# State-space layer of a four-layer kernel: residual added by the output product, normalization sums on ScalarE, an order of units changed

## The reference

```
h   = layernorm(xn) * g + b                    # 256 channels
xi, z = split(h @ W_in.T)                      # 512 channels each
u   = silu(causal conv over 4 tokens of xi)
dt, B, C = split(u @ W_x.T);  dt = softplus(dt @ W_dt.T + b_dt)
state[t] = exp(dt*A) * state[t-1] + dt*u*B     # 512 channels x 16 states
y   = (sum over states of state*C + u*D) * silu(z)
x   = x + (xn + y @ W_out.T)
```

## Time and profile before

| what | value |
|---|---|
| median of three runs | 2292.87 us |
| the profiled execution | 2300.35 us |
| its span | 2298.60 us |
| TensorE, VectorE, ScalarE, GpSimd busy in the span | 84%, 74%, 52%, 62% |
| the state-space layer's scans | 1081.7 to 1983.8 us |

### The profile page before, as it was taken

The page is one execution under the profiler, slowest core; times in us unless marked ns, Lnnn a source line. Parts: engine busy times, 40 slices in busy tenths (PEclk is TensorE's granted clock), DMA queues, the critical chain, the costliest instruction groups (busy, mean ns, idle before and its releaser), DMA issues. The chain is left out here.

```text
span 2298.6 us, 32626 instructions
## 1 busy us (share of the span) xinstructions
PE 1941.0 (84%) x9846; PEld 1136.6 (49%) x9846; DVE 1694.2 (74%) x2406; ACT 1198.6 (52%) x2466; POOL 1430.1 (62%) x1164
## 2 busy tenths in 40 slices
PE   2499999999873999947989898989898987569998
PEld 1234444444433999933444444444444433257776
DVE  4488777787744656522999999999999999655654
ACT  1066666666652433325676767676767574223222
POOL 7334435543342444422999999999999999444444
PEclk9699989898876999978999999999999999879999
DMA  3554444453143544424040404040404040101110
GB/s 81 103 110 101 103 96 108 111 124 100 51 153 127 100 70 75 76 39 157 0 148 19 148 19 148 19 148 19 148 19 148 10 148 9 60 7 37 36 36 19
DMA packets 231216, 185.57 MB, mean 81 GB/s; under 512 B 148729, under 2 KB 201601, under 8 KB 231058
## 3 DMA queue, kind: packets, MB, share of 16 engines
q1 hardware_dynamic: 216178, 162.61, 25.1%
q0 software_dynamic: 13296, 17.77, 4.4%
q10 hardware_dynamic: 1584, 3.24, 0.4%
HBM read 134.07 MB, written 49.49 MB: 80 GB/s over the span
## 5 line engine op out<-in xcount | busy, mean ns | idle before, releaser
L1769 POOL TENSOR_TENSOR mb_dbu<-mb_dtu,mb_bbc 128x1024 f32<-128x1024 f32 x256 | 600.4, 2361 | 41.8 <-DVE mb_hp L1900 29.6
L473 ACT ACTIVATE ex_plain<-at_t_ps 128x512 f32<-128x512 f32 x512 | 289.4, 595 | 185.9 <-PE at_t_ps L851 180.7
L1902 DVE TENSOR_TENSOR_SCAN mb_da_ps<-mb_da_ps,mb_dbu 128x1024 f32<-128x1024 f32 x160 | 365.3, 2283 | 12.6 <-ACT mb_da_ps L1819 12.6
L1953 PE MATMUL mb_y_ps<-mb_hc,lw_ident 128*128 128x512 f32 x640 | 323.9, 631 | 57.2 <-DVE mb_hc L1908 57.2
L610 DVE TENSOR_REDUCE at_mx<-at_s_ps 128x2 f32<-128x1024 f32 x256 | 310.8, 1219 | 51.4 <-PE at_s_ps L860 49.1
L860 PE MATMUL at_s_ps<-ex_w 48*128 48x512 f32 x512 | 228.1, 507 | 38.4 <-DVE at_mx L610 24.9
L851 PE MATMUL at_t_ps<-ex_w 64*128 64x512 f32 x512 | 221.7, 490 | 12.6 <-ACT ex_plain L473 6.7
L1953 PEld LDWEIGHTS mb_y_ps<-mb_hc,lw_ident 128*128 128x128 f32 x640 | 123.7, 199 | 215.7 <-issue 127.0
L1775 POOL TENSOR_TENSOR mb_hp<-mb_hp,mb_cbc 128x1024 f32<-128x1024 f32 x96 | 226.6, 2361 | 0.0
L1211 POOL DMA_INDIRECT x<-m_o,m_xs x71 | 113.7, 1602 | 172.8 <-DMA x<-m_o,m_xs 111.5
L1900 DVE TENSOR_TENSOR_SCAN mb_hp<-mb_da_ps,mb_dbu 128x1024 f32<-128x1024 f32 x96 | 218.8, 2279 | 2.5 <-ACT mb_da_ps L1819 2.5
(11 more groups left out here) (317 smaller groups left out, 4107.7 us busy)
## 6 DMA issues: line engine op xcount, KB each, us to landing
mb_bbc<-mb_scr SPq DMA_DIRECT2D x64, 512.0 KB, 5.4
mb_cbc<-mb_scr SPq DMA_DIRECT2D x64, 512.0 KB, 4.7
ex_w<-at_scr SPq DMA_DIRECT2D x384, 64.0 KB, 2.3
m_xs<-rt_rows SPq DMA_DIRECT2D x71, 129.0 KB
at_scr<-at_qk_hi SPq DMA_DIRECT2D x32, 256.0 KB
at_scr<-at_qk_lo SPq DMA_DIRECT2D x32, 256.0 KB
at_xin<-in_x SPq DMA_DIRECT2D x32, 128.0 KB, 2.3
ex_plain<-in_x SPq DMA_DIRECT2D x8, 512.0 KB
```

Source lines behind the costliest of these rows:

```text
L473: act.activation(probs[:, c, h, :], t_ps[:, k % 2, :], ACT.Exp, scale=SCALE).then_inc(exp_done, 1)
L1769: pool.tensor_tensor(dbu[:, q % 3, :, :], dtu_2, bbc[:, 2 * p:2 * p + 2, :], ALU.mult).then_inc(S["dbu_ready"], 1)
L1902: dve.tensor_tensor_scan(da, da, add, 0.0, ALU.mult, ALU.add).then_inc(S["scan_done"], 1)
L1953: last = pe.matmul(y_ps[:, v % 2, :], ident[:, :], src[:, j, :], start=False, stop=(q == tile_last[v] and j == 1))
```

## The change

The output product of a token tile begins with identity times the residual rows, so that PSUM holds the sum; ScalarE copies it to `res` two slots after the product, where VectorE added it three slots after. The statistics of a batch are now taken by ScalarE tile by tile, in slots 10 to 13 of the table instead of all in slot 11: a copy scaled by 1/256 with a sum over the row (the mean), a copy of the mean times -1/16, and the square of x/16 - mean/16 with a sum over the row (the variance). What the two wide instructions write goes to `res` and is overwritten later by norm_r. They wait for the store of the batch that last used this part of `res`. In the table xi 1 moves from slot 0 of the next batch to 31, xi 0 from 31 to 30, z 3 from 26 to 24 and both tr from 27 to 26; the tables of the first two batches keep the earlier order, except that xi 1 of the second batch stands in slot 1. `POOL_UNITS` names the same units as `POOL_PAIRS` did.

```diff
--- before.py
+++ after.py
@@ -1621,22 +1621,22 @@
 NP = DS // 2
 NU = ND * NP
 
-POOL_PAIRS = (1, 3, 5)
+POOL_UNITS = tuple(q for q in range(NU) if q % NP in (1, 3, 5))
 
 SCHEDULE = {
-    0: [("xi", 1, 1)], 1: [("dt", 1, 0)], 2: [("out_a", 0, -1)], 3: [("out", 0, -1)], 4: [("out_a", 1, -1)], 5: [("out", 1, -1)],
-    6: [("conv_a", 0, 1), ("final", 0, 0)], 7: [("conv", 0, 1)], 8: [("dt", 2, 0), ("load", 0, 2)], 9: [("conv_a", 1, 1)], 10: [("conv", 1, 1)],
-    11: [("xi", 2, 1), ("ln", 0, 2)], 12: [("xi", 3, 1)], 13: [("z", 0, 1), ("newton", 0, 2)], 14: [("conv_a", 2, 1), ("final", 1, 0), ("rsqrt", 0, 2)],
+    1: [("dt", 1, 0)], 2: [("out_a", 0, -1)], 3: [("out", 0, -1)], 4: [("out_a", 1, -1)], 5: [("out", 1, -1)],
+    6: [("conv_a", 0, 1), ("final", 0, 0)], 7: [("conv", 0, 1)], 8: [("dt", 2, 0), ("load", 0, 2)], 9: [("conv_a", 1, 1)], 10: [("conv", 1, 1), ("ln", 0, 2)],
+    11: [("xi", 2, 1), ("ln", 1, 2)], 12: [("xi", 3, 1), ("ln", 2, 2)], 13: [("z", 0, 1), ("ln", 3, 2), ("newton", 0, 2)], 14: [("conv_a", 2, 1), ("final", 1, 0), ("rsqrt", 0, 2)],
     15: [("conv", 2, 1)], 16: [("dt", 3, 0)], 17: [("conv_a", 3, 1), ("norm_r", 0, 2)], 18: [("conv", 3, 1)], 19: [("silu_u", 0, 1)],
-    20: [("norm_h", 0, 2)], 21: [("z", 1, 1)], 22: [("xd", 0, 1), ("final", 2, 0)], 23: [("z", 2, 1)], 24: [("scr", 0, 1), ("bb", 0, 1), ("bb", 1, 1)],
-    25: [("dt", 0, 1), ("bb", 2, 1), ("cb", 0, 1)], 26: [("z", 3, 1), ("bb", 3, 1), ("cb", 1, 1)], 27: [("tr", 0, 2), ("tr", 1, 2), ("bb", 4, 1), ("cb", 2, 1)],
-    28: [("silu_z", 0, 1), ("bb", 5, 1), ("cb", 3, 1)], 29: [("bb", 6, 1), ("cb", 4, 1)], 30: [("final", 3, 0), ("bb", 7, 1), ("cb", 5, 1)],
-    31: [("xi", 0, 2), ("cb", 6, 1), ("cb", 7, 1)],
+    20: [("norm_h", 0, 2)], 21: [("z", 1, 1)], 22: [("xd", 0, 1), ("final", 2, 0)], 23: [("z", 2, 1)], 24: [("scr", 0, 1), ("z", 3, 1), ("bb", 0, 1), ("bb", 1, 1)],
+    25: [("dt", 0, 1), ("bb", 2, 1), ("cb", 0, 1)], 26: [("tr", 0, 2), ("tr", 1, 2), ("bb", 3, 1), ("cb", 1, 1)], 27: [("bb", 4, 1), ("cb", 2, 1)],
+    28: [("silu_z", 0, 1), ("bb", 5, 1), ("cb", 3, 1)], 29: [("bb", 6, 1), ("cb", 4, 1)], 30: [("xi", 0, 2), ("final", 3, 0), ("bb", 7, 1), ("cb", 5, 1)],
+    31: [("xi", 1, 2), ("cb", 6, 1), ("cb", 7, 1)],
 }
-LATER = (("z", 0, 1), ("z", 1, 1), ("z", 2, 1), ("z", 3, 1), ("norm_h", 0, 2), ("silu_z", 0, 1))
-MOVED = {24: LATER[4:5], 25: LATER[0:2], 26: LATER[2:4]}
-EARLY_SCHEDULES = {-1: {at: [task for task in SCHEDULE[at] if task not in LATER] + list(MOVED.get(at, ())) for at in SCHEDULE},
-                   0: {at: SCHEDULE[at] + [("silu_z", 0, 0)] * (at == 1) for at in SCHEDULE}}
+MOVED = {24: [("norm_h", 0, 2)], 25: [("z", 0, 1), ("z", 1, 1)], 26: [("z", 2, 1), ("z", 3, 1)], 27: [("tr", 0, 2), ("tr", 1, 2)], 31: [("xi", 0, 2)]}
+LATER = [task for at in MOVED for task in MOVED[at]] + [("xi", 1, 2), ("silu_z", 0, 1)]
+EARLY_SCHEDULES = {-1: {at: [task for task in SCHEDULE[at] if task not in LATER] + MOVED.get(at, []) for at in SCHEDULE},
+                   0: {at: [("xi", 1, 1)] * (at == 1) + SCHEDULE[at] + [("silu_z", 0, 0)] * (at == 1) for at in SCHEDULE}}
 FILL_KINDS = ("out", "z", "dt", "tr", "xi", "conv", "xd")
 
 
@@ -1650,7 +1650,7 @@
         zero1 = sb("zero1", [P, 1])
         xin = sb("xin", [P, 4, D])
         res = sb("res", [P, 3, 4, D])
-        stats, mv = sb("stats", [P, 4, 6]), sb("mv", [P, 4, 2])
+        mv, nm = sb("mv", [P, 4, 2]), sb("nm", [P, 4])
         av, lv, rs, tv, nb = (sb(q, [P, 2, 4]) for q in ("av", "lv", "rs", "tv", "nb"))
         up = sb("up", [P, 4])
         hT_hi, hT_lo = (sb(f"hT_{s}", [P, 2, T], F32R) for s in ("hi", "lo"))
@@ -1669,7 +1669,7 @@
         y_ps = ctx.enter_context(nc.psum_tensor("mb_y_ps", [P, 2, T], F32))
         f_ps = ctx.enter_context(nc.psum_tensor("mb_f_ps", [P, 2, T], F32))
 
-        names = """prep a_exp x_stored const_set x_loaded stats_done var_ready a_made ln_done rs_ready
+        names = """prep a_exp x_stored const_set x_loaded stats_done a_made ln_done rs_ready
                    newton norm_ready h_ready f_ready hT_hi_ready z_ready u_ready scr_written ex_steps ex_ready dt_steps dtu_ready
                    da_ready dbu_ready scan_done hc_ready hp_ready y_summed yg_ready"""
         S = {q: sem("mb_" + q) for q in names.split()}
@@ -1699,11 +1699,11 @@
             eng.wait_ge(f_used[k % 2], k // 2 + 1)
 
         def by_pool(q):
-            return q % NP in POOL_PAIRS
+            return q % NU in POOL_UNITS
 
         def turn(q):
 
-            return sum(by_pool(v) == by_pool(q) for v in range(q % NP)) + (q // NP) * (len(POOL_PAIRS) if by_pool(q) else NP - len(POOL_PAIRS))
+            return sum(by_pool(v) == by_pool(q) for v in range(q % NU)) + (q // NU) * (len(POOL_UNITS) if by_pool(q) else NU - len(POOL_UNITS))
 
         def multiplied(eng, q):
 
@@ -1818,8 +1818,16 @@
                         act.activation(da_ps[:, q % 2, 0, :], dt[:, d % 2, :], ACT.Exp, scale=a_neg[:, d, 2 * p:2 * p + 1])
                         act.activation(da_ps[:, q % 2, 1, 1:T], dt[:, d % 2, 1:T], ACT.Exp, scale=a_neg[:, d, 2 * p + 1:2 * p + 2]).then_inc(S["da_ready"], 1)
                     for kind, i, m in tasks(s - 2):
+                        if kind == "ln":
+                            act.wait_ge(S["x_loaded"], 16 * (m + 1))
+                            wait(act, S["x_stored"], 16 * (m - 2))
+                            act.activation(res[:, m % 3, i, :], xin[:, i, :], ACT.Copy, scale=1.0 / D, accum_out=mv[:, i, 0:1]).then_inc(S["stats_done"], 1)
+                            act.wait_ge(S["stats_done"], 12 * m + 3 * i + 1)
+                            act.activation(nm[:, i:i + 1], mv[:, i, 0:1], ACT.Copy, scale=-1.0 / 16.0).then_inc(S["stats_done"], 1)
+                            act.wait_ge(S["stats_done"], 12 * m + 3 * i + 2)
+                            act.activation(res[:, m % 3, i, :], xin[:, i, :], ACT.Square, scale=1.0 / 16.0, bias=nm[:, i:i + 1], accum_out=mv[:, i, 1:2]).then_inc(S["stats_done"], 1)
                         if kind == "rsqrt":
-                            act.wait_ge(S["var_ready"], m + 1)
+                            act.wait_ge(S["stats_done"], 12 * m + 12)
                             act.activation(av[:, 0, :], mv[:, :, 1], ACT.Identity, bias=fix[:, 0:1]).then_inc(S["a_made"], 1)
                             act.activation(av[:, 1, :], mv[:, :, 1], ACT.Identity, scale=1.0 + 1e-6, bias=fix[:, 1:2]).then_inc(S["a_made"], 1)
                             act.wait_ge(S["a_made"], 2 * m + 2)
@@ -1862,6 +1870,9 @@
                                     last = act.activation(z[:, part[0]:part[1], :], z[:, part[0]:part[1], :], ACT.Silu)
                             last.then_inc(S["z_ready"], 1)
                             act.preload_act_table_set("natural_log_exp_and_others")
+                        if kind == "out":
+                            f, used = filled(act, "out", i, m)
+                            act.activation(res[:, m % 3, 2 * i:2 * i + 2, :], f.rearrange("p (a c) -> p a c", a=2), ACT.Copy).then_inc(used, 1)
                         if kind == "xd":
                             f, used = filled(act, "xd", 0, m)
                             wait(act, S["scr_written"], 16 * m)
@@ -1912,15 +1923,6 @@
                             dve.wait_ge(S["y_summed"], tile_summed[v])
                             dve.wait_ge(S["z_ready"], m + 1)
                             dve.tensor_tensor(u[:, m % 2, i, :], y_ps[:, v % 2, :], z[:, v % 5, :], ALU.mult).then_inc(S["yg_ready"], 1)
-                        if kind == "ln":
-                            dve.wait_ge(S["x_loaded"], 16 * (m + 1))
-                            wait(dve, S["h_ready"], m)
-                            for k in range(4):
-                                dve.bn_stats(stats[:, k, :], xin[:, k, :]).then_inc(S["stats_done"], 1)
-                            dve.wait_ge(S["stats_done"], 4 * m + 4)
-                            for k in range(4):
-                                last = dve.bn_aggr(mv[:, k, :], stats[:, k, :])
-                            last.then_inc(S["var_ready"], 1)
                         if kind == "tr":
                             f, used = filled(dve, "tr", i, m)
                             dve.wait_ge(S["hT_hi_ready"], 2 * m + i + 1)
@@ -1934,10 +1936,6 @@
                             dve.tensor_tensor(f, lg[:, :], f, ALU.subtract).then_inc(S["dt_steps"], 1)
                             dve.wait_ge(S["dt_steps"], 2 * v + 2)
                             dve.tensor_tensor(dt[:, i % 2, :], f, dt[:, i % 2, :], ALU.add).then_inc(used, 1)
-                        if kind == "out":
-                            f, used = filled(dve, "out", i, m)
-                            r_2 = res[:, m % 3, 2 * i:2 * i + 2, :]
-                            dve.tensor_tensor(r_2, f.rearrange("p (a c) -> p a c", a=2), r_2, ALU.add).then_inc(used, 1)
 
             @block.tensor
             def _(pe):
@@ -1985,8 +1983,9 @@
```

(3 more changed lines are left out.)

## The result

The changed kernel takes 2294.95 us (median of 20 runs, 2290.14 to 2299.07) where the kernel before takes 2291.55 (20 runs): ratio 1.0015, 95% interval 1.0008 to 1.0022. That is +3.4 us (the interval gives 1.8 to 5.0), slower than before by less than 0.2%; the forecast was +9.0.

What follows compares the result with a forecast made beforehand. VectorE was taken as the bound, with ScalarE and TensorE touching it at a few places. Terms beside the scans (+0.9) and outside (+8.1) summed to +9.0 us, giving 2301.9 us; range 2286 to 2312.

Steps and rivals of the forecast that it cites:

- first gate product, six batches: Second to seventh batch: extra output products on TensorE make each first gate product 0.53 us later, +3.2 us.
- second gate product: Statistics leaving VectorE gain 1.53 us in five batches, 1.73 in the first; the seventh loses 0.2: together -9.2 us.
- fourth gate product: In six batches the new order adds 2.7 us of TensorE work, exceeding the slack: +10.1 us, bounds nothing and 13.
- first scan to first gate product: First batch: xi 1 stands before dt 1 and the gate function in ScalarE's queue, where VectorE already waits: +0.6 us.
- first statistics: Before the scans, on the only path: ScalarE's four tiles take 5.4 us instead of VectorE's 1.7, +3.7 us.
- second statistics: Between conv 1 and the gate function: 5.4 us of sums less ScalarE's 2.7 us wait for TensorE, +2.7 us.
- Before the scans: Ahead of the first scan nothing covers ScalarE's sums, so two batches' statistics cost +3.7 and +2.7 us.
- sign that I named for a wrong forecast: First scan starting less than 3 us later, or VectorE's waits at the fourth gate product being absent.
- (a): Projections hide at the fourth gate product because the half-clock spell is short: the 10.1 us go, 2291.8; chance 0.2.
- (b): Modelled matmul ends hide larger slack at the first and fourth gate products: some -10 us, 2282.8; chance 0.13.
- (c): ScalarE's read-outs dear, 1.8 us a tile, and a longer half-clock spell on TensorE: +10 us, 2312; chance 0.17.
- (d): Moving z 3 two units sooner does nothing, running in TensorE's idle time at the bank: costed at nothing; no chance given.

Runs made afterwards that it cites:

- e1: The changed kernel with the order of units put back as before; sums on ScalarE and residual on TensorE stay: 2284.84 us, ratio 0.9973.
- e2: The kernel before with only the statistics sums moved to ScalarE; order and residual as before: 2280.71 us, ratio 0.9956.
- e5: The changed kernel with z 3 and both tr back in their earlier slots; only xi 0 and xi 1 sooner: 2290.69 us, ratio 0.9994.
- e6: The changed kernel with xi 0 and xi 1 back in their earlier slots; only z 3 and tr sooner: 2291.87 us, ratio 0.9998.
- e7: The changed kernel with the residual added by VectorE as before, without identity products or ScalarE's copies: 2289.43 us, ratio 0.9990.
- e10: The changed kernel with the first two batches' statistics back on VectorE: 2294.33 us, ratio 1.0004.
- e4: The kernel before with only the new order of units; statistics and residual stay on VectorE: 2305.35 us, ratio 1.0065.
- e8: The kernel before with sums on ScalarE only for the six batches beside the scans; the first two stay on VectorE: 2281.46 us, ratio 0.9949.
- e11: The kernel of e8 measured once more, nothing changed: 2281.87 us, ratio 0.9947 to the kernel before.

## Why the prediction was partly right

The direction was right, and so was the place of nearly every gain and loss. The size was wrong: the sum, +9.0, was 4.1 us above the layer's +4.93 and 5.6 above the medians' +3.4. The time lies in the range; of the two outcomes that 0.2% separates, "same" came, which had 0.22. By the prediction's own terms:

| term | forecast | measured |
|---|---|---|
| first gate product, six batches | +3.2 | 6 x 0.56 = +3.4 |
| eighth batch | -1.2 | -1.2 |
| second gate product | -9.2 | -10.3 |
| small waits at the third | -2.6 | -3.1 |
| fourth gate product | +10.1 | +8.9 |
| first scan to first gate product | +0.6 | +1.7 |
| first statistics | +3.7 | +3.2 |
| second statistics | +2.7 | +2.1 |
| from there to the first scan | nothing | -1.4 |
| end | +1.7 | +1.6 |
| sum | +9.0 | +4.9 |

**The step that failed** is the one of "Before the scans": "there nothing covers ScalarE", +3.7 and +2.7. It took ScalarE's delay to reach the first scan at its full length. Forecast +6.4, measured +3.9. Of the 2.5 us between them 1.1 are sizes: a tile was 0.08 us cheaper, VectorE's first statistics had held the path 1.9 us instead of 1.7 (1019.51 to 1021.45 in the trace of before), and the second sums delayed the gate function by 2.1 us. The other 1.4 us are a term that I put at nothing: TensorE's clock on the path from the gate function to the first scan. The eight instructions of xd, the table of stretches, before and after:

```profile
1057.67:1063.86 6.19, 6.18 (x8) 1.41 (x8) 0.00 (x0) 1.16 (x1) 0.00 (x0) 0.58 0.00 0
1052.33:1057.76 5.43, 5.43 (x8) 1.29 (x8) 0.00 (x0) 1.15 (x1) 0.00 (x0) 0.66 0.00 0
```

The same work takes 6.19 us at a granted clock of 0.58 and 5.43 at 0.66, and the z projections behind it take 0.7 us less as well (0.63 and 0.72). The change edits neither. This is not one execution's chance: in the six kernels with the first sums on ScalarE (after, e1, e2, e5, e6, e7) TensorE stands idle 6.1 us before xd, xd takes 5.09 to 5.44 us and the first scan comes 25.6 to 26.0 us after the gate function's table load; in the seven others it is idle 4.4 us, xd takes 6.19 to 6.43 and the distance is 27.4 to 27.7. Why the clock is higher after the longer wait was not tried. So, against before, the sums cost 5.2 - 1.9 us at the first batch, 1.6 to 2.1 at the second, and 1.4 to 1.8 come back on the way to the first scan. e10 gives the part of the sums as a whole, 3.5 us. Within one kind the starts still differ by up to 1 us (69.02 to 70.00, 66.05 to 66.68).

With that step two others were mis-sized: the fourth gate product 1.2 us too dear and the second 1.1. A term of 1.1 us was missing on the other side, below; that it nearly cancels the 1.4 us is luck.

**The fourth gate product.** The added work, +2.7 us at the full clock, was right to the tenth. The slack I set against it was the mean over the batches of before, and contains their spells (27.2 us in six); after had 25.2, which is 1.0 of the 1.2 us that I was too high. The upper bound of 13 us, for longer spells, was right in kind and in size: e4, with the same order and spells that are 5.4 us longer in sum than before, pays 12.7 us there.

**The second gate product.** The forecast of -1.53 a batch was -1.66 in four batches and -2.03 in the fifth, and nothing was lost in the seventh, where I had put +0.2.

**First to first.** In the first batch xi 1 ahead of dt 1 costs VectorE 0.6 us, as forecast (e4 and e10: +0.57). In after another 1.1 us comes with the sums, a wait of 1.00 at the gate product among it. It is TensorE's clock again. After its last wait before this product TensorE has the same instructions in after and in e10; timeline and table of stretches, after first:

```profile
1101.01 3.78 PE L1951 MATMUL mb_y_ps<-mb_hc,lw_ident 128*128 128x512 f32 x4 [3.83 <-DVE mb_hc L1919]
1104.58 3.19 PE L1974 MATMUL mb_f_ps<-mb_xi,lw_diag 128*128 128x512 f32 x4
1104.00:1107.00 3.00, 3.00 (x4) 1.08 (x4) 2.90 (x3) 1.39 (x3) 3.00 (x3) 0.50 0.02 5
...
1102.54 3.45 PE L1964 MATMUL mb_y_ps<-mb_hc,lw_ident 128*128 128x512 f32 x4 [3.83 <-DVE mb_hc L1923]
1105.82 1.88 PE L1987 MATMUL mb_f_ps<-mb_xi,lw_diag 128*128 128x512 f32 x4
1105.54:1108.54 3.00, 3.00 (x8) 1.32 (x8) 2.90 (x3) 1.39 (x3) 3.00 (x3) 1.00 0.00 0
```

The wait is the same 3.83 us, but the convolution behind it takes 3.19 us at 0.50 instead of 1.88 at 1.00. The lower clock lasts 5.9 to 6.2 us here in the three kernels that have both the first sums on ScalarE and xi 1 sooner (after, e5, e7) and 2.9 to 3.4 in the ten others, and only those three wait at this gate product.

**What the profile was to show.** L1940 and the statistics are gone from VectorE, and a tile is 1.27 us (1.3 to 1.5 named). The aside that cheaper tiles would lower the sum by 1.5 us was too small: before the scans the sum holds eight tiles, so 0.25 to 0.45 us off each make 2.0 to 3.6. VectorE's wait at the gate product is 21.2 us (about 26 named, though the parts named beside it and the last wait make 25.2): 1.00 and six of 1.66 at the first, none at the second where I named five, six of 0.68 to 1.35 at the fourth, 3.8 at the end. TensorE's wait at the transposes is 6.7 us a batch (7.6), and the first scan comes 3.9 us later (6). Neither sign that I named for a wrong forecast appeared.

**Rivals.** (a), the projections hide, fell: the waits at the fourth gate product are there in all six batches. It nearly holds for either move alone (0.2 us there in e5, 0.9 in e6). (b), modelled ends hide a larger slack, fell: waits begin where the modelled slack ends, at 0.03 to 0.04 us, and interval less half the spell is 27.5 within 0.03 us over 18 batches. (c), dear read-outs and longer spells, fell for this kernel with 1.27 us a tile; its longer spell, which costs 3 us there, is real in e4 (2.7). (d) stays open: z 3 was moved only together with the transposes, never alone.

## What to carry to other kernels

Taking work off the bounding engine pays by the slack of the next one at that place: the same 1.2 us a batch were worth nothing with 0.36 us of slack behind them and 1.2 us where a convolution was missing, and the 1.73 us of the statistics were worth all of it. Slack is shared: two moves that cost 0.2 and 2.7 us alone cost 8.8 together, so measure a bundle's parts both alone and removed. And place decides for the lender too: sums on ScalarE are free beside the scans and cost 3.5 us before them, where nothing runs beside. A later start of the same products can also meet another clock: a delay of 5.3 us before the first scan arrived there as 3.9.

## What the runs showed of the hardware

- After the same wait at the same instruction TensorE's granted clock stayed at 0.50 for 2.7 to 6.0 us, depending on the batch. In one program it repeats from one execution to another (e8 and e11, on two chips, within 0.1 us), but an edit elsewhere shifts it: 18.1 us in six batches in e7, 32.6 in e4. In e10 the lengths of after come one batch later (5.9 3.8 2.7 5.6 in the third to sixth batch, 6.0 3.8 2.7 5.6 in the second to fifth of after), so a length does not belong to a batch's own work. What sets it within these ends was not tried.
- These spells move a batch by 1.6 us, and e4 against e7 by 7.3, 0.3% of the span but more than the whole effect of the change. The Trainium skill ("TensorE: Matmul & The Clock Gate", Part 1) says that the point of rise varies from run to run and advises not to fit a model to it, as its cost is under 1% of a typical span. The 0.3% agree with the size; in e8 and e11 it did not vary.
- A read-out of a row sum is an instruction of its own on ScalarE, ACTIVATION_READ_ACCUMULATOR, 0.19 us, and the square with a pointer as bias takes 0.51 us at 256 columns against 0.40 for the copy.
- Phases that are the same in both kernels put the start of the layer 10.7 us apart in two profiled executions, three times the measured effect. Over the thirteen profiled executions it lies between 1001.2 and 1015.7 us.
